# Perceiver attention: the place of the next scores in TensorE's order of work

## The reference

```
q = latents @ Wq            # 512 x 1024, per batch
k, v = kv @ Wkv             # (512 + 77) rows, 16 heads of 64
s = q k^T * 64**-0.5        # masked keys out
p = softmax(s)              # per head, 512 x 589
o = p v                     # 512 x 64 per head
```

## Time and profile before

| | |
|---|---|
| median of 3 runs | 3330.24 us |
| the profiled execution | 3332.2 us |
| its span (first to last instruction) | 3330.4 us |
| mean granted TensorE clock | 0.938 |
| PE matmul busy | 2998.8 us (90%) |
| PE weight load busy | 2522.2 us (76%) |
| DVE busy | 2078.5 us (62%) |
| ACT busy | 1557.5 us (47%) |
| POOL busy | 1324.4 us (40%) |
| perceiver, steady part | 1131 to 2634 us |

### The profile page before, as it was taken

One profiled execution on the slowest core, in us unless ns is written; L12 is line 12 of the kernel. 1 busy time (PEld: TensorE's weight loads), 2 busy tenths in 40 slices (PEclk: granted clock), 3 DMA queues, 4 the chain that ended last, 5 costly groups with the idle time before them and its releaser, 6 DMA issues. The chain is left out here.

```text
span 3330.4 us, 44846 instructions
## 1 busy us (share of the span) xinstructions
PE 2998.8 (90%) x16620; PEld 2522.2 (76%) x16620; DVE 2078.5 (62%) x4123; ACT 1557.5 (47%) x3036; POOL 1324.4 (40%) x913
## 2 busy tenths in 40 slices
PE   6888999967675799999999999999999769999998
PEld 5777777745333798989899898989989657777776
DVE  4766666632357677777777777777777654444442
ACT  2333333321024576767767676777767522222222
POOL 2444444420012355565656565655555421111110
PEclk9999999987776899999999999999999879999999
DMA  5112111113059212121211212121121331111100
GB/s 181 36 46 60 51 49 40 47 38 139 0 189 365 79 41 60 37 63 40 62 34 36 65 36 63 38 70 31 38 63 34 107 101 51 51 51 51 51 26 26
DMA packets 131550, 220.43 MB, mean 66 GB/s; under 512 B 44749, under 2 KB 46798, under 8 KB 127245
## 3 DMA queue, kind: packets, MB, share of 16 engines
q1 hardware_dynamic: 120237, 187.42, 18.3%
q10 hardware_dynamic: 11104, 30.23, 2.3%
HBM read 112.01 MB, written 69.47 MB: 54 GB/s over the span
## 5 line engine op out<-in xcount | busy, mean ns | idle before, releaser
L1644 POOL TENSOR_SCALAR pa_Pr<-pa_Pr,pa_rs 128x590 f32<-128x590 f32 x512 | 903.1, 1768 | 647.5 <-DVE pa_rs L1866 647.4
L1870 DVE TENSOR_REDUCE pa_least<-pa_S 128x1 f32<-128x590 f32 x512 | 390.7, 763 | 192.0 <-PE pa_S L1708 189.8
L1821 DVE TENSOR_TENSOR pa_PTl<-pa_W,pa_PTh 128x512 fp32r<-128x512 f32 (+1 forms) x640 | 421.1, 683 | 26.1 <-ACT pa_PTh L1769 18.1
L1800 ACT ACTIVATE pa_Pr<-pa_S,pa_least 128x590 f32<-128x590 f32 x512 | 384.8, 752 | 100.3 <-DVE pa_least L1870 97.0
L1769 ACT ACTIVATE pa_PTh<-pa_W 128x512 fp32r<-128x512 f32 (+1 forms) x640 | 367.4, 596 | 115.1 <-PE pa_W L1719 98.4
L1719 PE MATMUL pa_W<-pa_ident,pa_Pr 128*128 128x128 f32 (+1 forms) x2560 | 365.5, 273 | 0.7 <-DVE pa_U L1821 0.6
L1719 PEld LDWEIGHTS pa_W<-pa_ident,pa_Pr 128*128 128x128 f32 (+1 forms) x2560 | 303.9, 142 | 23.3 <-DVE pa_U L1821 0.8
L1733 PE MATMUL pa_O<-pa_PTh,pa_V 128*128 128x512 f32 (+1 forms) x640 | 288.4, 451 | 12.3 <-DVE pa_PTl L1821 8.1
L1734 PE MATMUL pa_O<-pa_PTl,pa_V 128*128 128x512 f32 (+1 forms) x640 | 252.7, 395 | 0.0
L1706 PE MATMUL pa_S<-pa_U,pa_Qh 128*128 128x296 f32 (+1 forms) x1024 | 228.1, 304 | 5.5 <-DMA pa_Um<-pa_U 5.2
L1708 PE MATMUL pa_S<-pa_Um,pa_Ql 128*128 128x296 f32 (+1 forms) x1024 | 222.8, 299 | 0.0
(11 more groups left out here) (400 smaller groups left out, 7236.7 us busy)
## 6 DMA issues: line engine op xcount, KB each, us to landing
pa_Um<-pa_U SPq DMA_DIRECT2D x128, 147.5 KB
pa_Qh<-pa_Qh SPq DMA_DIRECT2D x128, 128.0 KB
o_s<-pa_O_pair SPq DMA_DIRECT2D x64, 256.0 KB, 2.6
ex_o_raw<-o_s SPq DMA_DIRECT2D x8, 2048.0 KB, 10.7
z_s<-la_z_hi ACTq DMA_DIRECT2D x8, 1180.0 KB, 7.2
z_s<-la_z_lo ACTq DMA_DIRECT2D x8, 1180.0 KB, 9.5
pa_z_hi<-z_s SPq DMA_DIRECT2D x8, 1180.0 KB, 5.7
pa_z_lo<-z_s SPq DMA_DIRECT2D x8, 1180.0 KB, 8.4
```

Source lines behind the costliest of these rows:

```text
L1644: pool.tensor_scalar(p, p, rs[:, g % 2, t:t + 1], None, ALU.mult).then_inc(*pool_s.mark("probs", n))
L1800: act.activation(Pr[g % 2][:, t, :], scored[n % 2], ACT.Exp, scale=-1.0, bias=least[:, g % 2, t:t + 1], accum_out=rs[:, g % 2, t:t + 1]).t ...
L1821: dve.tensor_tensor(out, src, f32(hi_ap), ALU.subtract).then_inc(*dve_s.mark(*name))
L1870: dve.tensor_reduce(least[:, g % 2, t:t + 1], scored[n % 2], AX, ALU.min).then_inc(*dve_s.mark("least", n))
```

## The change

Two moves in TensorE's loop in build_perceiver; no instruction is added or taken away, and the loops of the other engines are not touched. The scores of step n + 1 are issued behind W3 and W4 (t = 0), behind T0 and T1 (t = 1), and behind T2 and W0, ahead of T3 and W1 (t = 2); at t = 3 they are still first. The early value pieces are issued behind all of the step's transposes and weighings. Since the banks of the ring W are chosen from TensorE's order, some transposes and value pieces get another bank than before.

```diff
             for n in range(1 - LEAD, STEPS + 2 * NT + 1):
                 g, t = divmod(n, NT)
-                if 0 <= n + 1 < STEPS:
-                    scores(n + 1)
-                for q, j in v_at.get((n, True), []):
-                    value(q, j)
                 if t == 0:
                     weigh(g - 2, 3)
                     weigh(g - 2, 4)
...
                 if t == 2:
                     transposed(g - 1, 2)
                     weigh(g - 1, 0)
+                if 0 <= n + 1 < STEPS:
+                    scores(n + 1)
+                if t == 2:
                     transposed(g - 1, 3)
                     weigh(g - 1, 1)
                 if t == 3:
                     transposed(g - 1, 4)
                     weigh(g - 1, 2)
+                for q, j in v_at.get((n, True), []):
+                    value(q, j)
                 if q_of(n) is not None:
                     query(q_of(n))
```

## The result

The changed kernel takes 3505.02 us (median of 4 runs, 3504.21 to 3505.68) against 3330.49 us of the kernel before on the same chip (4 runs): 1.0529 times as long, 95% interval 1.0511 to 1.0547, or 175 us more. The forecast was 3485 us, with a range of 3435 to 3510.

A forecast was written before the change was run, and what follows sets the result against it. TensorE's queue was taken to set the pace; added waits of 56 + 89 + 9 + 1 = 155 us on the profiled 3332.2 us gave 3487.2, less 2.0 for the median: 3485 us, own range 3435 to 3510.

The forecast's parts named there:

- The bound: Perceiver's steady part: TensorE's queue sets the pace, busy 1479 of 1503 us; added waits come out at the end.
- Part 1: Step behind the query: minimum and low parts start 0.90 us later, W2 waits 1.25; 62 x 0.90 = 56 us.
- Part 2: Steps 4 to 6, behind the key: W0 loses its covers and waits 1.85 us; 48 x 1.85 = 89 us.
- The lower bound, 1.03: Least wait at W0 behind a key, in us, taken from the row that has no early V.
- Part 3: The 7 quads at a batch's edge: waits at W0, W4 and V banks; 7 x 1.3 = 9 us, bounds 0 to 15.
- What would show it: Signs in the changed profile, among them W's wait for the low part growing from 34 to about 180 us.
- The sign of 1.2 us at W2: Behind a query, the changed profile must show waits of 1.2 us at W2.
- A half of it: Rival, chance 0.10: VectorE makes up its lateness behind the key; 3386 us, or 3435 with the low bound.
- The clock: Rival, chance 0.10: TensorE's waits lower the perceiver's granted clock to 0.96, costing 62 us more: 3547.
- Faster: Rival, chance 0.03: ScalarE or a bank holds T2's low part behind the query, so the 34.2 us go: 3296.
- no change: Rival, chance 0.05: same work, TensorE full, chains with slack of 1.8 us between T0 and W0: 3330.
- What was said of the busy times: Sign in the changed profile: VectorE's and TensorE's busy times stay as before.

The follow-up runs named there:

- the second run: Only the early value pieces moved behind the transposes and weighings, scores still first, against the kernel before: 3382.13 us, ratio 1.0154.
- The first run: Only the scores of t = 2 moved behind T2 and W0, early values still in front, against the kernel before: 3421.04 us, ratio 1.0278.
- The fourth run: Only the scores of t = 0 and t = 1 moved, t = 2 and the early values as before, against the kernel before: 3357.88 us, ratio 1.0092.

## Why the prediction was right, and what was mis-sized

**The bound.** Right: TensorE's queue set the pace, its instructions were the same, and the loss is its waits, 179 us more in the list for 175 measured.

**Part 1, behind the query.** Right in mechanism and size: 0.90 forecast, 0.93 in the rows (4.53 less 3.60) and 0.91 in the mean of the 62 steps, 56 us for 56. It is shown by intervention: with VectorE's order changed in these steps alone 68 us come back: the 56 and the 22 that the kernel before lost there, less the new wait at W4 (0.12 in 62 steps) and a few us at the edges.

**Part 2, behind the key.** Right: a wait of 1.85 forecast, 1.90 measured, W0 at 3.66 behind the key's end (3.68 in the mean of the 48) where 3.61 was worked out; the delay of the key's low part was 0.32 (1578.00 less 1577.03, against 0.65 before), forecast 0.27. 48 x 1.90 = 91 for 89. The lower bound, 1.03, is what the values' move alone costs, as the second run shows; the scores' moves add the rest.

**Part 3, the edges, was sized too small, and so were the ends of the stage.** TensorE's pieces can be told apart in both timelines, so the 173 us between the two profiled executions can be laid out from key end to key end (a pair of heads each) and set against the 155 of the sum.

The 48 ordinary pairs take 2.92 us more in the mean, 140 us for 132 (48 times 0.90 + 1.85). An example: 25.76 (key ends 1551.27 and 1577.03) and 26.91 us (to 1603.94), 22.75 and 24.09 before (1508.65, 1531.40, 1555.49). The 8 us that no part had are the query behind a quad's values: it now waits for a V bank, 0.3 us in every other pair and 0.1 in the rest.

The 7 pairs at a batch's edge whose values come in step 13 take 3.3 more each, 23 us for 15; one is 30.85 us (key ends at 1520.42 and 1551.27; 27.48 before, 1291.00 to 1318.48). What the term left out is the value piece of step 14, which waits for V's bank as well (0.55 us of idle ahead of its start at 1528.41): VectorE reads V at 1527.67, behind the minimum at 1526.99, whose scores now stand behind T2 and W0.

The 7 pairs ahead of those take 23.6 us in the mean, 22.9 before: 0.7 more, 5 us for 6, as z's wait has all but gone and hides the rest. Ahead of the first and behind the last key the stage takes 1.2 and 3.6 us more, where 1 was given: with no values left, the last heads wait at W0 three times and at W4 twice, 0.6 to 0.9 us each. In all 140 + 23 + 5 + 5 = 173. The remaining 2 of the 20 us by which the forecast was short are the step from a profiled execution to the median: 2.0 was taken off, and 0.4 would have been right.

**What would show it.** The low part's wait at W was to grow to about 180 us; it is 103.6, and the rest stands one place earlier, at the claims of T4 (60.4) and T2 (35.6). The sign of 1.2 us at W2 wasn't met either: W2 itself waits 0.29 and T4 has the rest, which part 1 had said and this list of signs had not. The chains and their lengths were the ones forecast, only the instruction that the profile hangs the wait on was not.

**The rivals.** "A half of it" fell: VectorE's idle time did grow, but at the head of its queue, where it can't be used. "The clock" fell: the granted clock of the stretch is 1.00, and none of its pieces of 5 us from 1131 to 2806 us shows less, with TensorE idle for 0.73 us behind a query and for 0.38 and 1.03 us behind a key. But the prediction's ground for it, that the stage before held 1.00 through waits for z of up to 2.3 us, was misread from a mean. Behind the longest of these waits the clock did fall to its lower level, once:

```profile
2421.00:2426.00 5.00, 2.71 (x8) 2.14 (x9) 1.99 (x5) 1.57 (x4) 1.19 (x2) 0.79 0.19 73
2426.00:2431.00 5.00, 5.00 (x29) 4.32 (x28) 3.15 (x7) 3.27 (x8) 2.39 (x2) 0.87 0.23 52
```

```profile
2423.29 0.50 PE L119 MATMUL pa_W<-pa_z_hi,pa_Wq_hi 128*128 128x512 f32 x1 [2.30 <-DMA pa_z_lo<-z_s]
```

That query took 4.44 us (to 2427.73) where another takes 2.90. The changed kernel has nearly lost its waits for z (0.5 us), and no such fall shows in its perceiver. The frequent swings that the Trainium skill describes ("TensorE: Matmul & The Clock Gate", section "A second HAM failure mode: psum-queue depth-cycling") were seen in neither kernel's perceiver. "Faster" and "no change" fell with the sign; the wait that "faster" hoped to remove can be removed, but on VectorE (3307.55 us).

**What was said of the busy times** was right for VectorE (2078.5 to 2062.3 us) but not for TensorE, whose busy time rose from 2998.8 to 3039.3 us with the same instructions: a busy TensorE in this profile isn't a measure of work.

**The miss in the experiments.** The first run's expectation (3390, measured 3421) took T0 to T2 as a chain of data only. The list of waits names the ring's banks, and these follow from the order too: whoever comes third behind a key claims its bank. The fourth run's (3365, measured 3358) came near with a bank wait that isn't there.

## What to carry to other kernels

Before moving instructions in one engine's queue, write down the other engines' queues beside it: an instruction moved later holds up everything that stands behind its reader, here low parts that had nothing to do with the scores. In a full engine, work that already stands in front of a wait can be its cover (the early values: 54 us), but work moved there from behind may only move the wait down (the key ahead of T4: 3 us gained). Shortening the chain that is waited for gave more (the minimum behind one low part: 20 us). And bank rings count as dependencies whose partner changes with the order.

## What the runs showed of the hardware

Three things that I had not expected. TensorE's busy time in the profile grew by 40 us, with equal instructions and nearly equal clock (0.938 and 0.940 in the mean), where waits were put in. And the behaviour is regular enough to be added: three partial changes gave 93, 30 and 54 us where all together gave 175, and two gave 68 and 40 us where both gave 108. The third is in the trace before: behind 2.30 us of idle TensorE the granted clock read 0.79 and 0.87 in the next two pieces of 5 us, though the stretch of 1503 us around them reads 1.00.
